# Token routing of a mixture of experts: 16 scatters by slot replaced by an inverse found with matmuls and one gather for each tile

## The reference, cut to what matters

```python
logits = einsum('bsh,he->bse', x, w_router)          # 8 experts
probs = softmax(logits); sel = argmax(probs)
wgt = probs[sel]                                     # its share
for e in range(8):
    y = relu(xt @ w1[e] + b1[e]) @ w2[e] + b2[e]     # 256 -> 1024 -> 256
    out = out + ((sel == e) * wgt)[:, None] * y
x = x + out
```

## Time and profile before

| | us |
|---|---|
| median of three runs | 738.28 |
| the profiled execution's own time | 740.46 |
| its span, first to last instruction | 738.7 |
| gate_and_project | 164 to 208 |
| context_mlp | 456 to 557, its routing from 515.9 |
| experts | 557 to 738 |
| PE busy | 586.2 (79%) |
| DVE busy | 497.5 (67%) |
| POOL busy | 312.2 (42%) |
| ACT busy | 292.3 (40%) |
| mean granted TensorE clock | 0.896 of 2.4 GHz |

### The profile page before, as it was taken

One profiled execution on the slowest core, in us unless ns is written; L12 is line 12 of the kernel. 1 busy time (PEld: TensorE's weight loads), 2 busy tenths in 40 slices (PEclk: granted clock), 3 DMA queues, 4 the chain that ended last, 5 costly groups with the idle time before them and its releaser, 6 DMA issues. The chain is left out here.

```text
span 738.7 us, 12022 instructions
## 1 busy us (share of the span) xinstructions
PE 586.2 (79%) x3622; PEld 507.3 (69%) x3623; DVE 497.5 (67%) x960; ACT 292.3 (40%) x536; POOL 312.2 (42%) x261
## 2 busy tenths in 40 slices
PE   4578999964397999999999986777006989989985
PEld 4468888953275898888888874457004878867874
DVE  5598888857406889898889857574702566566562
ACT  2144445412035787787878830223100121111120
POOL 4335344427012443343444312045470295699144
PEclk9699999995599999999999998865556999999998
DMA  6112111100342313222131002833425034044000
GB/s 212 29 34 53 30 28 29 29 1 7 87 116 49 81 43 76 55 63 67 43 87 44 1 1 82 295 104 150 163 101 180 16 147 180 7 161 157 29 14 4
DMA packets 28727, 56.47 MB, mean 76 GB/s; under 512 B 4410, under 2 KB 15675, under 8 KB 26634
## 3 DMA queue, kind: packets, MB, share of 16 engines
q1 hardware_dynamic: 24810, 49.64, 22.4%
q0 software_dynamic: 1776, 4.23, 1.6%
q10 hardware_dynamic: 2096, 2.05, 0.9%
HBM read 31.58 MB, written 8.21 MB: 54 GB/s over the span
## 5 line engine op out<-in xcount | busy, mean ns | idle before, releaser
L880 POOL TENSOR_SCALAR h_p<-h_p,h_rs 128x1024 f32<-128x1024 f32 x64 | 72.1, 1126 | 131.9 <-DVE h_rs L972 131.8
L979 DVE TENSOR_REDUCE h_nmx<-h_psS 128x1 f32<-128x1024 f32 x64 | 78.1, 1221 | 22.3 <-PE h_psS L1070 21.0
L959 DVE TENSOR_TENSOR h_pTl<-h_psT,h_pTh 128x512 fp32r<-128x512 f32 x128 | 81.5, 678 | 4.4 <-ACT h_pTh L907 4.4
L907 ACT CAST h_pTh<-h_psT 128x512 fp32r<-128x512 f32 x128 | 69.3, 590 | 29.6 <-PE h_psT L1030 29.4
L929 ACT ACTIVATE h_p<-h_psS,h_nmx 128x1024 f32<-128x1024 f32 x64 | 72.2, 1128 | 17.7 <-DVE h_nmx L979 17.7
L1041 PE MATMUL h_psO<-h_pTh,h_vs 128*128 128x256 f32 x256 | 70.0, 307 | 3.1 <-DVE h_oT L967 2.3
L308 POOL TENSOR_TENSOR a_p<-a_p,a_rs 128x616 f32<-128x616 f32 x32 | 39.0, 1219 | 74.7 <-DVE a_rs L355 74.7
L1030 PE MATMUL h_psT<-ident,h_p 128*128 128x128 f32 x512 | 67.4, 273 | 1.3 <-DVE h_pTl L959 1.2
L1030 PEld LDWEIGHTS h_psT<-ident,h_p 128*128 128x128 f32 x512 | 59.2, 140 | 11.2 <-issue 3.3
L1041 PE MATMUL h_psO<-h_pTl,h_vs 128*128 128x256 f32 x256 | 63.7, 282 | 0.0
L1500 POOL TENSOR_TENSOR wl<-wst,wh 128x1024 fp32r<-128x1024 f32 (+1 forms) x18 | 56.0, 3110 | 2.7
(11 more groups left out here) (262 smaller groups left out, 1475.0 us busy)
## 6 DMA issues: line engine op xcount, KB each, us to landing
wst<-in_m_w SPq DMA_DIRECT2D x16, 1024.0 KB, 6.0
bias<-in_m_b SPq DMA_DIRECT2D x8, 640.0 KB, 8.8
h_kh<-h_hi SPq DMA_DIRECT2D x32, 128.0 KB, 2.4
h_kl<-h_lo SPq DMA_DIRECT2D x32, 128.0 KB, 2.4
rows<-c_blank SPq DMA_DIRECT2D x1, 3250.0 KB, 18.7
xg<-rows SPq DMA_DIRECT2D x1, 2990.0 KB, 11.1
a_qs<-a_qhi SPq DMA_DIRECT2D x16, 128.0 KB, 2.3
a_qs<-a_qlo SPq DMA_DIRECT2D x16, 128.0 KB, 2.3
```

The source lines that it names most:

```text
L880: pool.tensor_scalar(pr[:, u % 4], pr[:, u % 4], rs[:, u:u + 1], 0.0, ALU.mult, ALU.add).then_inc(pn_ready, 1)
L907: act.copy(pTh[u // QP % 2][:, hf * HK:(hf + 1) * HK, u % QP * P:(u % QP + 1) * P], psT[hf][:]).then_inc(pT_hi, 1)
L959: vec.tensor_tensor(pTl[u // QP % 2][part], psT[hf][:], pTh[u // QP % 2][part], ALU.subtract).then_inc(pT_lo, 1)
L979: vec.tensor_reduce(nmx[:, u:u + 1], psS[u % 2][:], AX.X, ALU.max, negate=True).then_inc(max_ready, 1)
```

## The change

1. **Gate.** POOL's four bias additions (L666) wait for all four normalised chunks and for `col_ready`, instead of each for its own chunk.
2. **Rows.** `x_all` rows carry only mean and rstd behind the features (`ROW = D + 2`), written there by the layer norm. SP writes the chunks of `x_all` to `rows` in token order as soon as each has its rstd; the blank fill, the 16 scatters and the load back go.
3. **Routing.** The softmax's division leaves the path; `oh` is found on the logits. The ranks with their sums over tiles come from 17 bf16 matmuls into one PSUM tile (`counts`), the first slot of each expert from one product with a triangle. Then DVE builds for each token its tile (`passed`, one of TG = 25) and its place in it (`here`, one of 128), and 16 float32 matmuls (128 x 128 by 128 x 50) give for each slot the token number plus one and the share (`inverse`). From these come `src` (the row to fetch), `dst` (the output row, out of range for an empty slot) and `share`.
4. **Gathers.** POOL fetches each tile's 128 rows by `gather(g)`, an indirect DMA from `rows` to `xg[:, g]`. All gathers count one semaphore, `landed`, and each waits until the one before has landed. Gather 0 is in `context_mlp`, 1 to 3 open POOL's list in `experts`, and gather g+3 stands at the head of iteration g, ahead of the split and of the output scatter. DVE's `normalise(g)` waits for tile g.
5. **Weights.** POOL's low parts of expert 1 (`low(4)` to `low(7)`) move from `context_mlp` to `experts`, behind gathers 1 to 3. SP's load of expert 3, which waits for the last of them, moves along.

The core of the diff:

```diff
-ROW = D + 4
+ROW = D + 2
...
             pool.wait_ge(bo_in, 16)
+            pool.wait_ge(xn_ready, NC)
+            pool.wait_ge(col_ready, 1)
             for n in range(NC):
-                pool.wait_ge(xn_ready, n + 1)
                 xc = x_all[:, n * CH:(n + 1) * CH, 0:D]
                 pool.tensor_tensor(xc, xc, bo[:].unsqueeze(1).to_broadcast([P, CH, D]), ALU.add).then_inc(bo_added, 1)
...
-            sp.wait_ge(cleared, 1)
-            sp.dma_start(t["rows"].rearrange("(g p) r -> p g r", p=P),
-                         blank[:].unsqueeze(1).to_broadcast([P, TG, ROW])).then_inc(t["rows_cleared"], 16)
-            for x in range(2, 4):
-                next_expert(sp, t, io, x)
-
-            sp.wait_ge(scattered, 16 * T)
-            rows = t["rows"].rearrange("(g p) r -> p g r", p=P)
-            sp.dma_start(t["xg"][:, 0:2], rows[:, 0:2]).then_inc(t["back"][0], 16)
-            sp.dma_start(t["xg"][:, 2:TG], rows[:, 2:TG]).then_inc(t["back"][1], 16)
+            rows = t["rows"].rearrange("(t p) r -> p t r", p=P)
+            for n in range(NC):
+                sp.wait_ge(rstd_ready, n + 1)
+                sp.dma_start(rows[:, n * CH:(n + 1) * CH], x_all[:, n * CH:(n + 1) * CH]).then_inc(stored, 16)
+            next_expert(sp, t, io, 2)
...
-            for i in range(2, 2 * NC):
-                low(i)
-
-            pool.wait_ge(t["rows_cleared"], 16)
-            pool.wait_ge(slot_ready, 1)
-            for i in range(T):
-                pool.indirect_dma_start(out=t["rows"], out_offset=bass.IndirectOffsetOnAxis(
-                    ap=slot[:, i:i + 1].bitcast(U32), axis=0), in_=x_all[:, i, :], in_offset=None,
-                    bounds_check=TG * P - 1, oob_is_err=False).then_inc(scattered, 16)
+            low(2)
+            low(3)
+            pool.wait_ge(stored, 16 * NC)
+            pool.wait_ge(src_ready, 1)
+            gather(pool, t, 0)
...
-            link(vec.tensor_copy(lg[:], psR[:]))
             full = [P, T, NE]
-            link(vec.tensor_reduce(best[:], lg[:], AX.X, ALU.max))
-            vec.tensor_tensor(e[:], lg[:], best[:].unsqueeze(2).to_broadcast(full), ALU.subtract).then_inc(shifted, 1)
-            vec.wait_ge(exp_done, 1)
-            link(vec.tensor_reduce(tot[:], e[:], AX.X, ALU.add))
-            link(vec.reciprocal(tot[:], tot[:]))
-            link(vec.tensor_tensor(e[:], e[:], tot[:].unsqueeze(2).to_broadcast(full), ALU.mult))
-            link(vec.tensor_reduce(x_all[:, :, D + 2], e[:], AX.X, ALU.max))
-
-            link(vec.tensor_tensor(first[:], e[:], x_all[:, :, D + 2:D + 3].to_broadcast(full), ALU.is_equal))
+            link(vec.tensor_reduce(best[:], psR[:], AX.X, ALU.max))
+            most = best[:].unsqueeze(2).to_broadcast(full)
+            link(vec.tensor_tensor(first[:], psR[:], most, ALU.is_equal))
             link(vec.scalar_tensor_tensor(first[:], first[:], -float(NE), num[:, 0:NE].unsqueeze(1)
                                           .to_broadcast(full), ALU.mult, ALU.add))
             link(vec.tensor_reduce(low[:], first[:], AX.X, ALU.min))
-            vec.tensor_tensor(oh[:], first[:], low[:].unsqueeze(2).to_broadcast(full), ALU.is_equal).then_inc(oh_ready, 1)
+            vec.tensor_tensor(oh[:, 0:T], first[:], low[:].unsqueeze(2).to_broadcast(full),
+                              ALU.is_equal).then_inc(oh_ready, 1)
+            vec.tensor_tensor(e[:], psR[:], most, ALU.subtract).then_inc(shifted, 1)
+
             vec.wait_ge(count_ps, 1)
-            vec.tensor_copy(rank[:], psC[:, 0])
-            link(vec.tensor_copy(scan[:, 0], psC[:, 1]))
-            a = 0
-            for d in (1, 2, 4, 8):
-                vec.tensor_copy(scan[:, 1 - a, 0:d], scan[:, a, 0:d])
-                link(vec.tensor_tensor(scan[:, 1 - a, d:T], scan[:, a, d:T], scan[:, a, 0:T - d], ALU.add))
-                a = 1 - a
-            vec.tensor_tensor(base[:], psC[:, 1], scan[:, a], ALU.subtract)
-            link(vec.tensor_scalar(steps[:], num[:, 0:T], float(P), None, ALU.mult))
-
-            link(vec.tensor_tensor(fits[:], scan[:, a, T - 1].unsqueeze(2).to_broadcast([P, NE, T]),
+            link(vec.tensor_tensor(fits[:], counts[:, T].unsqueeze(2).to_broadcast([P, NE, T]),
                                    steps[:].unsqueeze(1).to_broadcast([P, NE, T]), ALU.is_gt))
             link(vec.tensor_reduce(tiles[:], fits[:], AX.X, ALU.add))
-            link(vec.tensor_scalar(tiles[:], tiles[:], 1.0, None, ALU.max))
-            link(vec.tensor_copy(ends[:, 0], tiles[:]))
-            a = 0
-            for d in (1, 2, 4):
-                vec.tensor_copy(ends[:, 1 - a, 0:d], ends[:, a, 0:d])
-                link(vec.tensor_tensor(ends[:, 1 - a, d:NE], ends[:, a, d:NE], ends[:, a, 0:NE - d], ALU.add))
-                a = 1 - a
-            end = ends[:, a]
-            link(vec.tensor_tensor(tiles[:], end, tiles[:], ALU.subtract))
-            link(vec.tensor_scalar(tiles[:], tiles[:], float(P), None, ALU.mult))
-
-            link(vec.tensor_tensor(rank[:], rank[:], base[:], ALU.subtract))
-            link(vec.tensor_tensor(rank[:], rank[:], tiles[:].unsqueeze(1).to_broadcast(full), ALU.add))
-            link(vec.tensor_tensor(rank[:], rank[:], oh[:], ALU.mult))
+            link(vec.tensor_tensor(shares[:], tiles[:].unsqueeze(1).to_broadcast([P, NE, NE]), lower[:], ALU.mult))
+            link(vec.tensor_reduce(first_slot[:], shares[:], AX.X, ALU.add))
+            link(vec.tensor_tensor(rank[:], counts[:, 0:T], first_slot[:].unsqueeze(1).to_broadcast(full), ALU.add))
+            link(vec.tensor_tensor(rank[:], rank[:], oh[:, 0:T], ALU.mult))
             link(vec.tensor_reduce(slotf[:], rank[:], AX.X, ALU.add))
-            vec.tensor_copy(slot[:], slotf[:]).then_inc(slot_ready, 1)
-            link(vec.tensor_tensor(done_e[:], end[0:1].unsqueeze(1).to_broadcast([1, TG, NE]),
+            wide = [P, T, TG]
+            link(vec.tensor_tensor(passed[:], slotf[:].unsqueeze(2).to_broadcast(wide),
+                                   steps1[:].unsqueeze(1).to_broadcast(wide), ALU.is_ge))
+            link(vec.tensor_reduce(group[:], passed[:], AX.X, ALU.add))
+            vec.scalar_tensor_tensor(place[:], group[:], -float(P), slotf[:], ALU.mult, ALU.add)
+            vec.wait_ge(exp_done, 1)
+            link(vec.tensor_reduce(tot[:], e[:], AX.X, ALU.add))
+            vec.reciprocal(wgt[:], tot[:])
+            link(vec.tensor_tensor(passed[:], group[:].unsqueeze(2).to_broadcast(wide),
+                                   num[:, 0:TG].unsqueeze(1).to_broadcast(wide), ALU.is_equal))
+            for x, value in enumerate((tok1, wgt)):
+                ins = vec.tensor_tensor(sent[:, :, x], passed[:], value[:].unsqueeze(2).to_broadcast(wide), ALU.mult)
+            ins.then_inc(sent_ready, 1)
+            for n in range(NC):
+                part, box = slice(n * CH, (n + 1) * CH), [P, CH, P]
+                vec.tensor_tensor(here[:, part], num[:].unsqueeze(1).to_broadcast(box),
+                                  place[:, part].unsqueeze(2).to_broadcast(box), ALU.is_equal).then_inc(here_ready, 1)
+
+            vec.wait_ge(inv_ps, 1)
+            vec.tensor_scalar(src[:], inverse[:, 0], -1.0, 0.0, ALU.add, ALU.max).then_inc(src_ready, 1)
+            link(vec.tensor_scalar(empty[:], inverse[:, 0], 0.0, float(2 * B * S), ALU.is_equal, ALU.mult))
+            vec.scalar_tensor_tensor(dst[:], empty[:], -1.0, inverse[:, 0], ALU.add, ALU.add)
+            vec.tensor_copy(share[:], inverse[:, 1])
...
-            pe.matmul(psC[:, 0], before[:], oh[:], start=True, stop=True)
-            pe.matmul(psC[:, 1], ones[:], oh[:], start=True, stop=True).then_inc(count_ps, 1)
+            pe.matmul(counts, before[:], oh[:], start=True, stop=False)
+            for i in range(T):
+                ins = pe.matmul(counts[:, i + 1:], ones[:], oh[:, i].unsqueeze(1).to_broadcast([P, T - i, NE]),
+                                start=False, stop=(i == T - 1))
+            ins.then_inc(count_ps, 1)
+            pe.wait_ge(sent_ready, 1)
+            for i in range(T):
+                if i % CH == 0:
+                    pe.wait_ge(here_ready, i // CH + 1)
+                ins = pe.matmul(inverse, here[:, i], sent[:, i], start=(i == 0), stop=(i == T - 1))
+            ins.then_inc(inv_ps, 1)
...
+            for g in range(1, 4):
+                pool.wait_ge(landed, 16 * g)
+                gather(pool, t, g)
+            for i in range(NC, 2 * NC):
+                split_low(pool, t, t["w_high"], i)
             for g in range(1, MT + 1):
+                if g + 3 < TG:
+                    pool.wait_ge(landed, 16 * (g + 3))
+                    gather(pool, t, g + 3)
...
+                upto(vec, landed, g, 16, 16)
...
+def split_low(pool, t, w_high, i):
+
+    x, q = divmod(i, NC)
+    part = quarter(q)
+    pool.wait_ge(w_high, i + 1)
+    pool.tensor_tensor(t["wl"][:, x, part], t["wst"][:, x, part], t["wh"][:, x, part],
```

(61 more changed lines are left out.)

70 lines of the change are left out of this document (36 added, 34 removed).

## The result

The changed kernel takes 740.95 us (median of 11 runs, 739.85 to 744.16), the kernel before 737.18 beside it (11 runs). The ratio is 1.0059, with a 95% interval of 1.0039 to 1.0080: some 4 us slower, where 1.2 us faster was forecast. The profiled executions are 744.16 after and 740.46 before; their spans, 742.4 and 738.7, differ by 3.7.

What follows compares the result with a forecast made beforehand. No engine was full (PE 79% busy), so the chain of waits was taken as the bound. Gate -5.1, routing -19.2, experts' stage +23.1 gave -1.2 us: 739.3 for the profiled execution, 737 for the median, range 723 to 750.

Steps and rivals of the forecast that it cites:

- Gate: Gate's normalisations: with POOL's bias additions out of the way, the sum starts near 177.1 instead of 182.2, -5.1 us.
- Routing: Router's last product to first expert tile: new counts and products replace scatters and load back, 21.9 us, -19.2 us.
- E: The moment expert work starts on the first tile; forecast at 537.8 instead of 557.0, before the gate's 5.1.
- Place 1: Start of experts' stage: gathers 5 and 6 delay the split for expert 2, low parts cost PE nothing; +2.3 us.
- Place 2: Tile 8: gather 8, issued under a fresh expert load, lands late and delays PE's transposes; +6.8 us.
- Clock: Experts' stage: PE's idle time at tile 8 lowers its granted clock once, slowing 24 products; +1.8 us.
- Place 3: Experts 4 and 5: gather 12 ahead of a split, then gather 14 waiting for gather 13's slow landing; +8.5 us.
- place 4: Tile 16: gather 15 delays gather 16, which lands without a load beside it; +2.4 us.
- 5, end of the span: End of experts' stage: gather 22 stands ahead of the last split on POOL; +1.3 us.
- the late landings: Rival: experts' stage gathers land only when the expert's load is through; +16.6 us, 754 us, chance 0.16.
- the quick ones: Rival: experts' stage gathers land quickly even under a load, with no clock term; -13.3 us, 725 us, chance 0.31.
- 204 to 206 from first `e_xn` to the end: Sign in the experts' stage: this time would be 204 to 206 us instead of 181.8; below 195 meant quick landings.

Runs made afterwards that it cites:

- gate_alone: The kernel before with only the gate's bias additions on POOL moved behind all normalised chunks; 731.13 us, ratio 0.9902 to the kernel before.
- lows_back: The changed kernel with expert 1's four low parts back in `context_mlp` and expert 3's load waiting for gather 3; 734.38 us, ratio 0.9941.
- two_sems_first: split_first with two semaphores for even and odd gathers, each waiting for the one before the last; 714.35 us, ratio 0.9680.
- loads_later: The changed kernel with SP's loads of experts 3 to 7 waiting until the next gathers have landed; 735.78 us, ratio 0.9965.
- two_sems_look6: look6 with two semaphores for even and odd gathers; 717.05 us, ratio 0.9707 to the kernel before.
- look6: lows_back with gathers 1 to 6 ahead of the loop, gather g+6 in iteration g, and expert 3's load waiting for gather 6; 734.82 us, ratio 0.9950.
- split_first: look6 with each iteration's split ahead of its gather, and the gather ahead of the output scatter; 733.47 us, ratio 0.9939.
- two_sems: The changed kernel with two semaphores for even and odd gathers, each waiting for the one before the last; 729.86 us, ratio 0.9891.

## Why the prediction was wrong, step by step

The sum was -5.1 - 19.2 + 23.1 = -1.2. The traces give -5.6 - 20.2 + 29.5 = +3.7. The last term is the one that failed.

**Gate: right.** -5.6 for -5.1, by the mechanism named (POOL's additions held DVE up). The sum was forecast at 177.1; with the 0.7 us ahead of it, 175.88 is 0.5 earlier than that. gate_alone shows that the gain stands for itself.

**Routing: right.** 20.9 us for 21.9. The counts were taken at 2.8 us and cost 1.2; the 16 products were taken at 6.8 and cost 7.0.

Of these counts the Trainium skill, "TensorE: Matmul & The Clock Gate", section "Weight-path perf modes", says that weights which are not float32 and fill 128 columns are read several elements at a time. The traces agree: 0.07 us for each of the 17 instructions in bf16, 0.17 for each of the 34 in float32. The prediction's lower bound, 1.7 us for the 17, was still above the 1.2 measured.

**The experts' stage, place by place.** Each row gives when the same instruction begins in both kernels, counted from E, and what is new in the difference since the row before.

| place, and the instruction | before | after | forecast | measured |
|---|---|---|---|---|
| 1, split for expert 2 | 30.4 | 36.2 | +2.3 | +5.8 |
| 2, transposes of tile 8 | 62.8 | 75.9 | +6.8 | +7.3 |
| clock behind it, `hidden(8)` | 67.1 | 82.0 | +1.8 | +1.8 |
| 3, second half of `hidden(12)`, expert 5 | 101.7 | 124.2 | +8.5 | +7.6 |
| 4, transposes of tile 16 | 126.8 | 152.2 | +2.4 | +2.9 |
| clock behind it, `hidden(16)` | 131.1 | 158.8 | 0 | +2.3 |
| 5, end of the span | 181.7 | 211.2 | +1.3 | +1.8 |

**Place 1, the start: the step that failed.** The text said that what the low parts hold DVE up "hides before `hidden(1)`", and put the start at +2.3. It was +5.8. One DVE instruction in the middle of a chain waits for all four of POOL's: 8.77 us for a normalisation of 0.41, with the bias of tile 1 behind it in DVE's list, which PE's transposes wait for. So PE begins the transposes of tile 2 at E + 19.2 instead of 15.9, 3.3 us later. The granted clock is then 0.50, and the 24 products behind take 5.3 us (550.90 to 556.18) instead of 3.0 (573.02 to 575.98), which is 2.3 more. The row that gave the price of the hold was there: eight normalisations in 9.92 us beside POOL's additions. It was used for the gate and not here. The +2.3 itself was put down to gathers 5 and 6 waiting under the load of expert 3, and that did not come: both were issued straight behind a scatter (559.28 and 565.98) and landed in 2.9 and 2.8 us. lows_back shows the cause: 0.40 us, and the split at E + 30.7.

**Place 2, tile 8: right.** Gather 8 took 7.2 us, with DVE waiting, as forecast.

**Place 3, experts 4 and 5: right in the main.** Gathers 13 and 14 are 7.2 us apart, as forecast, and the split for expert 5 is later by 7.5. The 1.3 us for gather 12 ahead of the split for expert 4 did not come (0.2): that split waits for PE in the kernel after, not for POOL.

**Clock: the second step that failed.** One fall was forecast in this stage, and it came at its price, 1.8 us. Behind place 4 another came that the sum had at nothing: with 3.4 us of idle PE ahead of it, 24 products took 5.3 us (683.86 to 689.14) instead of 3.0, and `hidden(16)` is 2.3 us later for it. The one at the start cost 2.3 as well. The one at 648 cost nothing, since PE waits for POOL there before and behind it. These prices are read from the windows and the products in them; no experiment took the clock away by itself. In two_sems_first, where PE's long waits are gone, the falls between 548 and 700 us are gone too.

So the start is 3.5 us more than forecast, the clock behind place 4 2.3, places 2, 4 and 5 0.5 each, and place 3 0.9 less: 6.4 in all. Gate and routing gave 1.5 of it back. Of the rivals, the late landings did not come (7.2 us, not 10.9), nor the quick ones: the long landing under a load was right, and loads_later shows its cause. That the forecast "204 to 206 from first `e_xn` to the end" holds 205.4 for lows_back is in part luck: the start was +0.3 there and not +2.3, and its profiled execution lies 5.2 us above the median.

**Where the 20 us of the routing went** is shown by two_sems_look6 and two_sems_first. The scatters cost 19 us once. On the way to E only gather 0 is left of the transfers (landed 3.1 us after its issue), but inside POOL's list each waits for the landing of the one before, and SP's load begins just when POOL is through with a split and issues. This turned into late tiles (after), into late splits (look6), until the wait was gone: of 29.5 us given back 2.7 are left, by single traces. The expectations of look6 and split_first missed because they took the late tile for the cause; those edits moved the same wait to another engine.

## What to carry to other kernels

When a transfer is moved into an engine's instruction list, ask what the instruction waits for, besides how long it takes: here the 1.3 us of each gather were affordable, and the wait for the landing before it was not. Give each transfer in flight its own semaphore before fetching further ahead; alone, neither more distance nor another order helped. Four instructions of POOL in a row can cost a DVE instruction from SBUF to SBUF what is left of all four, so ask which single DVE instruction falls beside them and what is queued behind it.

## What the runs showed of the hardware

A DVE normalisation that started behind the first of four POOL instructions was not let in between them: 0.41 us became 8.77, through four `TENSOR_TENSOR` that followed one another without a gap. Only instructions that read and write SBUF alone were held so. In two_sems POOL's four run from 533.49 to 542.83; DVE's timeline beside them:

```profile
536.73 0.69 DVE L1596 SCALAR_TENSOR_TENSOR e_hl<-e_psT,e_hh 128x512 fp32r<-128x512 f32 x1
537.63 0.69 DVE L1596 SCALAR_TENSOR_TENSOR e_hl<-e_psT,e_hh 128x512 fp32r<-128x512 f32 x1 [0.21 <-ACT e_hh L1546]
538.23 4.75 DVE L1562 TENSOR_SCALAR e_xn<-xg 128x256 f32<-128x256 f32 x1
```

The two that read PSUM take their usual 0.69; the one from SBUF to SBUF ends 0.16 us behind POOL's last.

Not every boundary is closed. In the kernel before, `c_first` (518.46, 2.23 us instead of 0.29) ends 0.15 us behind the first of two low parts in a row, not behind the second. In the kernel after, a normalisation beside a split ends at 574.74, 0.15 us behind POOL's `TENSOR_TENSOR` (572.23, 2.37 us), though POOL goes straight on with a `TENSOR_SCALAR`:

```profile
573.47 1.27 DVE L1557 TENSOR_SCALAR e_xn<-xg 128x256 f32 x1
```

```profile
574.56 1.96 POOL L1501 TENSOR_SCALAR wh<-wst 128x2048 fp32r<-128x2048 f32 x1
```

What decides whether DVE gets in at a boundary, no run here shows.

The Trainium skill, "SBUF — State Buffer", section "SBUF: two separate sides", says that a DVE instruction in a two-port mode and one of GpSimd exclude each other, and that whichever starts first has the shared port for the whole instruction. The traces agree in that an instruction of DVE waits to the end of one of POOL's, and those that read PSUM do not. They show more: at the three boundaries between POOL's four the waiting normalisation did not get in (8.77 us), at the two boundaries above DVE did.

A gather of 128 rows of 1 KB lands in 6.0 to 7.2 us when SP's load of an expert has just begun (582.77, 599.17, 638.95, 663.38 in the kernel after), in 2.9 late in a load (646.12), and gather 8 in 3.0 where loads_later keeps the load away.
